# Convolution of the state-space layer: four full products against four half-width products of two taps each

## The chip, the cores and the metric

One core of one Trainium2 chip runs the whole kernel. The metric is the device time of one execution in microseconds (us); lower is better. All data are f32.

## The reference

The input is `x` of 8 sequences, 512 steps, 256 features. Two layers follow each other, each `x = x + s * silu(ffn-like gate)`. The first layer holds the part that changes: a bidirectional state-space block (both directions `d`) beside a mixture of experts.

```
xz = (hidden @ W_in.T).transpose(0, 2, 1)            # per sequence: 1024 channels x 512 steps
x, z = split(xz)                                      # 512 channels each
x = silu(conv(x, conv_w, padding left 3, per channel) + conv_b)     # 4 taps
x_dbl = x @ Wx.T ;  dt = softplus(x_dbl[:64] @ Wdt.T + bdt) ; B, C = rest
h[t] = exp(dt[t] * A) * h[t-1] + dt[t] * B[t] * x[t]  # 512 channels x 16 states
y[t] = C[t] . h[t] + x[t] * D ;  out = y * silu(z)
out_b: the same on the reversed sequence with weights of its own
```

The convolution is per channel: each output is the sum of four shifted inputs, each with one weight. The second layer (linear attention, a three-level MLP, a low-rank gate) is not touched.

## The kernel before

The kernel has three blocks that follow each other: the routing of the experts (first 84 us of the profile), the block with the state-space layer and the experts (84 to about 2,210 us), and the second layer.

In the middle block each sequence `b` has two **units**, `d = 0` (forward) and `d = 1` (backward). A unit has 16 steps `n`, one for each state, and each step has two halves `j`, so 32 **slots** `s = 2n + j`. The order on every engine is written out by hand, slot by slot, and the engines meet at semaphores:

- GpSimd (POOL) makes `dt*B*x` for one state into one of four buffers `hs` (L708), and for two of the 16 states also multiplies by C and adds (L677, L690, L694).
- ScalarE (ACT) makes the decay `exp(dt*A)` into PSUM (`decay`, L797: two instructions per slot, three steps ahead). It may begin only when VectorE has finished the scan that used that half's PSUM buffer.
- VectorE (DVE) runs the scan of a half (L884), two steps ahead, and then adds two turned chunks, weighed by C, to the result (`weigh`, L894).
- TensorE (PE) turns the finished states (`turn`, L1013: transposes into the PSUM banks `hT`), and VectorE's L894 reads them.

Beside this, in chosen slots (`PREP`), TensorE and ScalarE prepare the next unit. While a `d = 1` unit runs, the next sequence's forward unit is prepared: `proj` (L981) in slots 0, 1, 6, 7, each one block `k` of 128 channels, `conv` (L987) in slots 2, 4, 8, 10, then `silu`, `xd`, `dt`. While a `d = 0` unit runs, `conv` for the backward unit of the same sequence is in slots 4, 6, 7, 8 and there is no `proj` (slots 20 to 25 hold `gate`). The one PSUM bank `prep` serves all of these: TensorE waits, before it fills it, until ScalarE has read its last content (`pe.wait_ge(p_used, use)`). In a slot ScalarE's order is: decay, prepare, the expert tile's piece, `skip` (L805), output; TensorE's is: turn, prepare, the tile's piece.

`xpad` is the input of the convolution: 128 channels on the partitions, four blocks, 512 steps with three zeros on each side. ScalarE copies each `proj` result into it (L750). `taps` holds for each direction, block and tap a 128x128 matrix with the tap's weights on its diagonal, built by VectorE at the start of the block (L869). A block of the convolution is four products with the same PSUM target, one for each tap; the shift is the column at which `xpad` is read. The first unit is prepared ahead of all slots, in the same order, with four PSUM banks in turn (`first`).

Of the kernel before, what the change touches and what calls it, by code (L numbers as in the profile page):

```python
# [5 lines left out]
P = 128  # L6
NB, L, DM = 8, 512, 256
DI, NS, R, KC = 512, 16, 64, 4
# [8 lines left out]
DB = DI // P  # L17
HB = HE // P
HF = DB // 2
EPS = 1e-5  # L20
# [11 lines left out]
CW = 0  # L32
CB = CW + 2 * DB * KC
# [35 lines left out]
def bass_mamba_moe_then_linear_attention_mlp(nc, x, w_inT, w_xT, w_dtT, w_outT, cols0, rows0, w_rT, wl1, bl1c, wl2, bl2,  # L69
# [4 lines left out]
    ALU = mybir.AluOpType  # L74
    ACT = mybir.ActivationFunctionType
# [14 lines left out]
    with ctx:  # L90
# [9 lines left out]
        ident = sb("ident", [P, P])  # L100
# [97 lines left out]
        def s0(name, shape, dt=f32):  # L198
            return sb(name, shape, dt, lay0)
# [5 lines left out]
        cols = s0("cols", [P, NCOL0])  # L205
        xa = held[:, :].rearrange("p (c d) -> p c d", d=DM)
# [3 lines left out]
        w_sem = sem("weights_in")  # L210
        N_W = 6
# [5 lines left out]
        with layR:  # L217
# [21 lines left out]
            own = sr("own", [P, NT, NE])  # L239
# [13 lines left out]
            def _(sp):  # L253
# [16 lines left out]
                sp.dma_start(cols[:, :], cols0).then_inc(w_sem, 16)  # L270
                for d in range(2):
                    sp.dma_start(w_x[:, d, :, 0:RX], w_xT[d].rearrange("(k p) m -> p k m", p=P)).then_inc(w_sem, 16)
# [161 lines left out]
        with lay0:  # L434
            one_row = s0("one_row", [1, P])
            xnT = s0("xnT", [P, KD, L])
            xpad = s0("xpad", [P, DB, L + 2 * (KC - 1)])
# [7 lines left out]
            taps = s0("taps", [P, 2 * DB * KC, P])  # L445
# [21 lines left out]
            xnT_in, p_ps, p_used = sem("xnT_in"), sem("prep_ps"), sem("prep_used")  # L467
# [48 lines left out]
            assert N_USE == len(USES[1])  # L516

# [212 lines left out]
            def _(act):  # L730
# [13 lines left out]
                def prepare(what, k, d, unit, b=0, first=False):  # L744
# [4 lines left out]
                    if what == "proj":  # L749
                        nc.scalar.activation(xpad[:, k, KC - 1:KC - 1 + L], src[:, :], ACT.Copy).then_inc(p_used, 1)  # L750
# [110 lines left out]
            def _(dve):  # L861
# [95 lines left out]
            def _(pe):  # L957
# [4 lines left out]
                def prepare(what, k, d, unit, b, first=False):  # L962
# [19 lines left out]
                    elif what == "conv":  # L982
                        if first and k == 0:
                            pe.wait_ge(taps_ready, 2 * DB * KC)
# [630 lines left out]
```

## Time and profile before

| | us |
|---|---|
| median of 3 runs | 3241.3 (3237.01 to 3243.83) |
| the profiled execution, its own time | 3248.7 |
| its span, first to last instruction | 3246.9 |
| busy: PE / DVE / ACT / POOL | 2737.8 / 2252.4 / 1765.3 / 1754.2 |
| mean granted TensorE clock | 0.914 of 2.4 GHz |

Each engine works in its own order, and waits only where its next instruction needs a semaphore. Busy shares are means over three very different blocks, so they say little of one slot. A matmul of f32 appears as two records. In the rows, a bracket gives the idle time before an instruction and what ended it.

### The profile page before, as it was taken

To read this page: it belongs to the slowest core of one execution; us is meant where nothing else is said; L and a number is where in the kernel's file an instruction comes from. 1 tells how busy PE (TensorE), PEld (TensorE's weight loads), DVE (VectorE), ACT (ScalarE), POOL (GpSimd) and SP (SyncE) were. 2 spreads that over 40 slices of the span, in tenths; PEclk is the share of its full clock that TensorE was granted. 3 is DMA by queue.
4 is the path that set the end of the run, shared out by engine and by line. 5 is a ranking of instruction groups with operands and counts; after the bars stand their busy time and mean duration, and the time that the engine had idled before them with its cause. 6 is when DMAs were issued, how large, how long until landed. Compare 5 with 4: busy or idle time off the path is not lost. (4 is left out here: it accounts for less than half of the span.)

```text
span 3246.9 us, 40447 instructions
## 1 busy us (share of the span) xinstructions
PE 2737.8 (84%) x13486; PEld 1826.9 (56%) x13486; DVE 2252.4 (69%) x2812; ACT 1765.3 (54%) x2691; POOL 1754.2 (54%) x554
## 2 busy tenths in 40 slices
PE   5466887887888888878968878777999999999999
PEld 5134665665666565666656656555455555555554
DVE  5287989889889989989988988984442442442430
ACT  1355767758848758758758767641332332322322
POOL 0598868878878878778778887861000000000000
PEclk9777898899999989989989989887999999999999
DMA  6222324333333334333333332323000000000000
GB/s 254 85 69 94 119 101 140 108 109 119 123 106 121 107 104 147 109 105 117 129 115 115 111 134 90 130 89 131 26 33 0 32 32 0 32 18 15 6 7 7
DMA packets 149278, 283.24 MB, mean 87 GB/s; under 512 B 23659, under 2 KB 97878, under 8 KB 149078
## 3 DMA queue, kind: packets, MB, share of 16 engines
q1 hardware_dynamic: 142934, 264.08, 23.8%
q0 software_dynamic: 6144, 16.79, 1.5%
q8 instruction: 91, 1.49, 0.2%
q14 instruction: 109, 0.89, 0.1%
HBM read 239.13 MB, written 41.68 MB: 86 GB/s over the span
## 5 line engine op out<-in xcount | busy, mean ns | idle before, releaser
L708 POOL TENSOR_TENSOR hs<-u,bb 128x2048 f32<-128x2048 f32 x256 | 1159.3, 4534 | 368.5 <-PE hT L1013 323.3
L884 DVE TENSOR_TENSOR_SCAN hs<-dA,hs 128x1024 f32<-128x1024 f32 x512 | 1166.3, 2284 | 122.7 <-POOL hs L708 75.9
L797 ACT ACTIVATE dA<-dt,cols 128x511 f32<-128x511 f32 x1024 | 661.8, 680 | 412.9 <-DVE hs L884 408.6
L1013 PE MATMUL hT<-ident,hs 128*128 128x128 f32 x3584 | 558.4, 297 | 264.2 <-DVE held L894 222.4
L1013 PEld LDWEIGHTS hT<-ident,hs 128*128 128x128 f32 x3584 | 434.9, 151 | 405.6 <-DVE held L894 290.2
L894 DVE SCALAR_TENSOR_TENSOR held<-hT,ct,held 128x512 f32<-128x512 f32 x864 | 603.8, 742 | 54.2 <-PE hT L1013 53.1
L1287 ACT ACTIVATE gl<-bank,cols_sb 128x512 f32<-128x512 f32 x192 | 130.7, 687 | 528.4 <-PE bank L1526 528.1
L1526 PE MATMUL bank<-mT,cms_sb 128*128 128x512 f32 x768 | 363.6, 598 | 10.1 <-ACT mT L1281 8.6
L1032 PE MATMUL moe<-xgT,held 128*128 128x128 f32 x2400 | 334.4, 299 | 30.0 <-ACT xgT L811 28.2
L1032 PEld LDWEIGHTS moe<-xgT,held 128*128 128x128 f32 x2400 | 321.3, 214 | 61.4 <-ACT xgT L811 37.6
L136 POOL COPY cur<-slot 128x8 uint32 (+1 forms) x8 | 1.5, 187 | 640.9 <-DVE held L148 631.3
L1537 PE MATMUL bank<-gl,cms_sb 128*128 128x512 f32 x512 | 242.2, 600 | 7.3 <-issue 3.8
L1526 PEld LDWEIGHTS bank<-mT,cms_sb 128*128 128x128 f32 x768 | 144.4, 191 | 164.7 <-issue 147.5
L987 PE MATMUL prep<-xpad,taps 128*128 128x512 f32 x480 | 219.7, 600 | 2.7 <-ACT xc L758 2.7
L1038 PE MATMUL moe<-held,sa 128*128 128x256 f32 x600 | 178.8, 452 | 8.1 <-DVE sa L904 8.1
L1354 DVE TENSOR_TENSOR sm<-bank,mask 128x512 f32<-128x512 f32 x128 | 82.5, 686 | 137.0 <-PE bank L1421 136.2
L797 ACT ACT_TABLE_LOAD x131 | 168.1, 1283 | 3.7 <-issue 1.4
L1038 PEld LDWEIGHTS moe<-held,sa 128*128 128x128 f32 x600 | 136.6, 236 | 44.8 <-issue 16.2
L981 PE MATMUL prep<-xnT,w_in 128*128 128x512 f32 x248 | 134.8, 672 | 27.7 <-DMA xnT<-xnT_scratch 17.5
L1537 PEld LDWEIGHTS bank<-gl,cms_sb 128*128 128x128 f32 x512 | 92.9, 190 | 114.3 <-issue 101.2
L677 POOL TENSOR_TENSOR hs<-hs,cb 128x2048 f32<-128x2048 f32 x32 | 145.7, 4553 | 0.0
L987 PEld LDWEIGHTS prep<-xpad,taps 128*128 128x128 f32 x480 | 87.5, 192 | 91.8 <-issue 88.6
(219 smaller groups left out, 3332.1 us busy)
## 6 DMA issues: line engine op xcount, KB each, us to landing
held<-wl SPq DMA_DIRECT2D x75, 1024.0 KB
bb<-b_scratch SPq DMA_DIRECT2D x128, 512.0 KB, 5.6
held<-wl SPq DMA_DIRECT2D x75, 512.0 KB
xg_scratch<-zero SPq DMA_DIRECT2D x10, 960.0 KB, 5.4
xg<-xg_scratch SPq DMA_DIRECT2D x75, 128.0 KB
yg_scratch<-yg SPq DMA_DIRECT2D x75, 128.0 KB, 1.7
held<-x SPq DMA_DIRECT2D x16, 512.0 KB, 8.7
cb<-b_scratch SPq DMA_DIRECT2D x32, 256.0 KB, 4.7
```

What stands on the lines that cost most here:

```text
L677: nc.gpsimd.tensor_tensor(hs[m % HS][:, :, :], hs[m % HS][:, :, :], row, ALU.mult).then_inc(p_mul, 1)
L708: nc.gpsimd.tensor_tensor(hs[n % HS][:, :, :], u[d][:, :, :], row, ALU.mult).then_inc(dBu_ready, 1)
L797: last = nc.scalar.activation(dst, src, ACT.Exp, scale=cols[:, at:at + 1])
L884: nc.vector.tensor_tensor_scan(h, decay, h, 0.0, ALU.mult, ALU.add).then_inc(scan_done, 1)
L894: ins = nc.vector.scalar_tensor_tensor(out=yacc[:, c, :], in0=hT[c % 2][:, :], scalar=ct[d][:, c, n:n + 1], in1=yacc[:, c, :], op0=ALU.mul ...
L981: last = mm(dst[:, :], w_in[:, j, at:at + P], xnT[:, j, :], start=(j == 0), stop=(j == KD - 1))
L987: last = mm(dst[:, :], taps[:, (d * DB + k) * KC + t, :], xpad[:, k, at:at + L], start=(t == 0), stop=(t == KC - 1))
L1013: last = nc.tensor.transpose(hT[c % 2][:, k * P:(k + 1) * P], hs[n % HS][:, k, c * P:(c + 1) * P], ident[:, :])
L1032: last = mm(moe[:, m * P:(m + 1) * P], w1[r][:, k, (at + m) * P:(at + m + 1) * P], xgT[:, k, :], start=(k == 0), stop=(k == KD - 1))
L1038: mm(moe[:, 0:DM], sa[:, m, :], w2[r][:, m, :], start=(m == 0), stop=False)
L1526: last = mm(bank[4 + h % 2][:, :], cms1_sb[:, lv, k, h * P:(h + 1) * P], mT[lv][:, k, :], start=(k == 0), stop=(k == KD - 1))
L1537: last = mm(bank[6 + k][:, :], cms2_sb[:, lv, h, k * P:(k + 1) * P], gl[h % 2][:, :], start=(h == 0), stop=(h == HM - 1))
```

## The change

Each product now takes two taps and makes 64 output channels. The input is held twice: `xpad[g]` has on the 64 partitions of half `g` the channels of half `g`, and on the other 64 partitions the same channels, read one step on. A product over all 128 partitions with a 128x64 matrix of two diagonals so gives two taps. ScalarE writes all this from PSUM: four copies of 64 partitions each in place of one of 128. The two halves `g` write the PSUM partitions 0 to 63 and 64 to 127 of the same bank.

```
-            xpad = s0("xpad", [P, DB, L + 2 * (KC - 1)])
+            xpad = [s0(f"xpad{g}", [P, DB, L + 2 * (KC - 1)]) for g in range(2)]
-            taps = s0("taps", [P, 2 * DB * KC, P])
+            taps = s0("taps", [P, 2, DB, 2, KC // 2, HP])

                     if what == "proj":
-                        nc.scalar.activation(xpad[:, k, KC - 1:KC - 1 + L], src[:, :], ACT.Copy).then_inc(p_used, 1)
+                        for g in range(2):
+                            own, other = slice(HP * g, HP * (g + 1)), slice(HP * (1 - g), HP * (2 - g))
+                            nc.scalar.activation(xpad[g][own, k, KC - 1:KC - 1 + L], src[own, :], ACT.Copy)
+                            last = nc.scalar.activation(xpad[g][other, k, KC - 2:KC - 2 + L], src[own, :], ACT.Copy)
+                        last.then_inc(p_used, 1)

-                nc.vector.memset(xpad[:, :, 0:KC - 1], 0.0).then_inc(hT_used, 1)
-                nc.vector.memset(xpad[:, :, KC - 1 + L:], 0.0).then_inc(hT_used, 1)
+                for g in range(2):
+                    nc.vector.memset(xpad[g][:, :, :], 0.0).then_inc(hT_used, 1)
                 dve.wait_ge(w_sem, 16 * N_W)
-                for i in range(2 * DB * KC):
-                    nc.vector.tensor_scalar(taps[:, i, :], ident[:, :], cols[:, CW + i:CW + i + 1], None, ALU.mult).then_inc(taps_ready, 1)
+                for d in range(2):
+                    for k in range(DB):
+                        for g in range(2):
+                            for q in range(KC // 2):
+                                for half in range(2):
+                                    rows_ = slice(HP * half, HP * (half + 1))
+                                    at = (d * DB + k) * KC + tap_of(d, q, int(half != g))
+                                    nc.vector.tensor_scalar(taps[rows_, d, k, g, q, :], ident[rows_, rows_], w_tap[rows_, g, at:at + 1],
+                                                            None, ALU.mult).then_inc(taps_ready, 1)

-                        for t in range(KC):
-                            at = t if d == 0 else 2 * (KC - 1) - t
-                            last = mm(dst[:, :], taps[:, (d * DB + k) * KC + t, :], xpad[:, k, at:at + L], start=(t == 0), stop=(t == KC - 1))
+                        for q in range(KC // 2):
+                            at = pair_at(d, q)
+                            for g in range(2):
+                                last = mm(dst[HP * g:HP * (g + 1), :], taps[:, d, k, g, q, :], xpad[g][:, k, at:at + L],
+                                          start=(q == 0), stop=(q == KC // 2 - 1))
```

`pair_at(d, q)` gives the column at which pair `q` is read, and `tap_of` which tap's weight belongs to which half of the partitions. The weights on both halves come by four small loads into `w_tap` on SP's queue, in the routing block; the count of weight loads that the engines wait for at the start goes from 6 to 10. The number of products of a block stays four.

## Rows read from the trace of the kernel before

**Rows 1.** Page, part 1: busy us of the engines over the span.

```profile
PE 2737.8 (84%) x13486; PEld 1826.9 (56%) x13486; DVE 2252.4 (69%) x2812; ACT 1765.3 (54%) x2691; POOL 1754.2 (54%) x554
```

**Rows 2.** Costliest group by line: busy us, mean ns of one, idle before by releaser.

```profile
L884 DVE TENSOR_TENSOR_SCAN hs<-dA,hs 128x1024 f32<-128x1024 f32 x512 | 1166.3, 2284 | 122.7 <-POOL hs L708 75.9 <-ACT dA L797 33.5 <-issue 12.4
```

**Rows 3.** Waits from 400 to 2150 us: us in total, times, longest.

```profile
ACT xc L758 <- PE prep L987: 50.5, 46, 2.4
...
DVE held L894 <- PE hT L1013: 46.5, 48, 2.6
```

**Rows 4.** Line L750 by itself: ns min/median/max, first and last start.

```profile
L750 ACT ACTIVATE xpad<-prep x30: 574/597/602, 91.5 to 1849.1; 128x512 f32<-128x512 f32 x30
```

**Rows 5.** Timeline of ScalarE, 1316 to 1440 us (a `d = 1` unit), slots 0 to 10.

```profile
1320.77 0.60 ACT L750 ACTIVATE xpad<-prep 128x512 f32<-128x512 f32 x1 [0.61 <-PE prep L981]
1321.27 0.38 ACT L811 ACTIVATE xgT<-moe 128x256 f32<-128x256 f32 x1
...
1322.36 1.30 ACT L797 ACTIVATE dA<-dt,cols 128x511 f32<-128x511 f32 x2
1323.60 0.60 ACT L750 ACTIVATE xpad<-prep 128x512 f32<-128x512 f32 x1
...
1328.58 1.30 ACT L797 ACTIVATE dA<-dt,cols 128x511 f32<-128x511 f32 x2
...
1348.25 1.30 ACT L797 ACTIVATE dA<-dt,cols 128x511 f32<-128x511 f32 x2
...
1356.76 0.69 ACT L758 ACTIVATE xc<-prep,cols 128x512 f32<-128x512 f32 x1 [1.34 <-PE prep L987]
...
1380.84 1.30 ACT L797 ACTIVATE dA<-dt,cols 128x511 f32<-128x511 f32 x2 [0.88 <-DVE hs L884]
```

**Rows 6.** Timeline of VectorE in the same unit.

```profile
1325.83 1.41 DVE L894 SCALAR_TENSOR_TENSOR held<-hT,ct,held 128x512 f32<-128x512 f32 x2
...
1331.46 2.28 DVE L884 TENSOR_TENSOR_SCAN hs<-dA,hs 128x1024 f32<-128x1024 f32 x1
...
1344.80 2.29 DVE L884 TENSOR_TENSOR_SCAN hs<-dA,hs 128x1024 f32<-128x1024 f32 x1 [0.86 <-POOL hs L708]
1347.01 1.38 DVE L894 SCALAR_TENSOR_TENSOR held<-hT,ct,held 128x512 f32<-128x512 f32 x2
...
1351.81 2.28 DVE L884 TENSOR_TENSOR_SCAN hs<-dA,hs 128x1024 f32<-128x1024 f32 x1
```

**Rows 7.** Timeline of TensorE in the same unit.

```profile
1321.68 1.88 PE L981 MATMUL prep<-xnT,w_in 128*128 128x512 f32 x4
...
1325.19 1.04 PE L1013 MATMUL hT<-ident,hs 128*128 128x128 f32 x8
1326.06 3.60 PE L987 MATMUL prep<-xpad,taps 128*128 128x512 f32 x8
1329.50 1.03 PE L1013 MATMUL hT<-ident,hs 128*128 128x128 f32 x8
```

**Rows 8.** Timeline of TensorE in the last block, around a product group of 32 columns.

```profile
2505.04 1.88 PE L1526 MATMUL bank<-mT,cms_sb 128*128 128x512 f32 x4
2506.85 1.08 PE L1434 MATMUL bank<-sm,vp 128*32 128x128 f32 x32
2507.86 1.99 PE L1543 MATMUL bank<-cms_sb,gl 128*128 128x256 f32 x8
```

**Rows 9.** Timeline of 1210 to 1228 us, a `d = 0` unit.

```profile
1214.60 0.69 ACT L758 ACTIVATE xc<-prep,cols 128x512 f32<-128x512 f32 x1 [0.80 <-PE prep L987]
...
1215.80 1.29 ACT L797 ACTIVATE dA<-dt,cols 128x511 f32<-128x511 f32 x2
...
1227.23 2.29 DVE L884 TENSOR_TENSOR_SCAN hs<-dA,hs 128x1024 f32<-128x1024 f32 x1 [3.83 <-POOL hs L708]
```

**Rows 10.** Timeline of 84 to 94 us, the start of the block.

```profile
85.66 0.91 DVE L864 MEMSET dA<- 128x1024 f32 x1 [0.16 <-issue]
...
86.70 6.40 DVE L869 TENSOR_SCALAR taps<-ident,cols 128x128 f32<-128x128 f32 x31
```

More of the change, by code:

```diff
@@ L19 @@
 HF = DB // 2
+HP = P // 2
 EPS = 1e-5
@@ L205, in bass_mamba_moe_then_linear_attention_mlp @@
         cols = s0("cols", [P, NCOL0])
+        w_tap = s0("w_tap", [P, 2, CB])
         xa = held[:, :].rearrange("p (c d) -> p c d", d=DM)
@@ L210, in bass_mamba_moe_then_linear_attention_mlp @@
         w_sem = sem("weights_in")
-        N_W = 6
+        N_W = 10
         placed, zeroed, grouped = sem("placed"), sem("zeroed"), [sem("grouped_early"), sem("grouped_late")]
@@ L270, in _ @@
                 sp.dma_start(cols[:, :], cols0).then_inc(w_sem, 16)
+                for g in range(2):
+                    for half in range(2):
+                        sp.dma_start(w_tap[HP * half:HP * (half + 1), g, :], cols0[HP * g:HP * (g + 1), CW:CB]).then_inc(w_sem, 16)
                 for d in range(2):
@@ L516, in bass_mamba_moe_then_linear_attention_mlp, with pair_at, tap_of @@
             assert N_USE == len(USES[1])
+            def pair_at(d, q):
+                return 2 * q if d == 0 else 2 * (KC - 1) - 1 - 2 * q
+            def tap_of(d, q, early):
+                return pair_at(d, q) + early if d == 0 else 2 * (KC - 1) - pair_at(d, q) - early
             first_banks = [prep, moe, hT[0], hT[1]]
@@ L864, in _ @@
                     nc.vector.memset(dA[j][:, :, :], 0.0).then_inc(scan_done, 1)
-                nc.vector.memset(xpad[:, :, 0:KC - 1], 0.0).then_inc(hT_used, 1)
-                nc.vector.memset(xpad[:, :, KC - 1 + L:], 0.0).then_inc(hT_used, 1)
+                for g in range(2):
+                    nc.vector.memset(xpad[g][:, :, :], 0.0).then_inc(hT_used, 1)
                 dve.wait_ge(w_sem, 16 * N_W)
-                for i in range(2 * DB * KC):
-                    nc.vector.tensor_scalar(taps[:, i, :], ident[:, :], cols[:, CW + i:CW + i + 1], None, ALU.mult).then_inc(taps_ready, 1)
+                for d in range(2):
+                    for k in range(DB):
+                        for g in range(2):
+                            for q in range(KC // 2):
+                                for half in range(2):
+                                    rows_ = slice(HP * half, HP * (half + 1))
+                                    at = (d * DB + k) * KC + tap_of(d, q, int(half != g))
+                                    nc.vector.tensor_scalar(taps[rows_, d, k, g, q, :], ident[rows_, rows_], w_tap[rows_, g, at:at + 1],
+                                                            None, ALU.mult).then_inc(taps_ready, 1)
                 dve.wait_ge(setup_a, 1)
@@ L983, in prepare @@
                         if first and k == 0:
-                            pe.wait_ge(taps_ready, 2 * DB * KC)
-                        for t in range(KC):
-                            at = t if d == 0 else 2 * (KC - 1) - t
-                            last = mm(dst[:, :], taps[:, (d * DB + k) * KC + t, :], xpad[:, k, at:at + L], start=(t == 0), stop=(t == KC - 1))
+                            pe.wait_ge(taps_ready, 4 * DB * KC)
+                        for q in range(KC // 2):
+                            at = pair_at(d, q)
+                            for g in range(2):
+                                last = mm(dst[HP * g:HP * (g + 1), :], taps[:, d, k, g, q, :], xpad[g][:, k, at:at + L],
+                                          start=(q == 0), stop=(q == KC // 2 - 1))
                     elif what == "xd":
```

## The prediction

> **What bounds the kernel now.** I read the page's busy times first [rows 1]. No engine is full over the span, but TensorE at 84% leads, which would make a cheaper convolution look good. That share is a mean over three blocks, so I went to the groups by line. The dearest work of the middle block is VectorE's scan: 1166.3 us busy and only 122.7 us idle before it [rows 2]. The waits from 400 to 2150 us say who makes VectorE idle: TensorE's turned chunks cost it 46.5 us in 48 waits, while ScalarE's 50.5 us of waiting for the convolution [rows 3] is idle time of an engine that is not the bound by itself. So the question is not how much TensorE saves, but whether a slot of VectorE ends earlier or later. For that I read the timelines of one `d = 1` unit [rows 5 to 7] and one `d = 0` unit [rows 9]. A slot of VectorE is a scan and two weighed chunks, 3.5 us (from 1344.80 to 1351.81 are two slots) [rows 6], with almost nothing between. Thus anything that makes a decay or a turned chunk later than its slot stretches the unit, and anything that only makes TensorE earlier does nothing.
>
> **Convolution, cost of a block.** Now it is 8 records; the next turn starts 3.44 us after the first of them (1326.06 to 1329.50) [rows 7], so one record streams in 0.43 us. After the change it is again 8 records of 512 columns. The price hangs on whether the two halves run at once. The trace has no product of 64 columns, but it has one of 32, with four targets in turn: 32 records of 128 columns, and the next group starts 1.01 us after the first [rows 8]. A record of 128 columns one after the other would take 0.43/4 = 0.107 us, so 32 would take 3.4 us; the rows say 3.4 at a time out of four possible. Bounds: 8 x 0.43 = 3.44 us if the halves do not overlap, 4 x 0.43 = 1.72 us if they overlap fully. I take 1.8, since the row of the 32 columns is the same kind of product. Saving: 1.6 us for each of 64 blocks (16 units of four), 105 us of TensorE.
>
> A rule that speaks against this: the Trainium skill (TensorEngine Tiling (Array Packing), Key Properties) says that a change of the tiling mode drains TensorE, and each block now changes it twice. By the trace the change is small: the four records of 512 columns before the narrow group end their streaming at 2505.04 + 1.71 = 2506.75, and the group starts at 2506.85 [rows 8], so 0.1 us. With a drain as large as a record (0.43 us, twice) the saving would fall to 0.8 us a block, and the sum below would hardly move, because the saving is not on the path.
>
> **Copies of the input.** ScalarE writes four copies of 64 partitions where it wrote one of 128. One takes 597 ns [rows 4], and the instruction behind one starts 0.50 us after it (1320.77 to 1321.27) [rows 5]. All still have 512 elements for each partition. No row has a copy of 64 partitions, nor one that lands on other partitions. Bounds: 0.25 us each if the work went by partitions, 0.60 if nothing overlapped; I take 0.50, the row of the same length. So one `proj` costs 3 x 0.50 = 1.5 us more, 32 of them 48 us of ScalarE. Where do these lie? Four per forward unit, in slots 0, 1, 6, 7 of the `d = 1` unit before, seven times in the slots, and once ahead of them.
>
> **Slots 0 to 5 of a `d = 1` unit.** First copies at 1320.77: they end 1.5 us later, and the decay of slot 1 (1322.36) moves by 1.4. Its idle time before was 0.1. The second copies (1323.60) so start 1.4 late and end 2.9 late. Nothing on ScalarE between there and the decay of slot 2 waits for anything, so that decay starts at 1331.5 and ends at 1332.8 instead of 1329.9 [rows 5]. The scan that needs it ran at 1331.46 [rows 6]: it is 1.35 us late. On TensorE, the second `proj` (1321.68) needs the bank that the first copies have to leave: it moves to 1322.9, by 1.2 us, and the turn behind it with it (1325.19) [rows 7]. VectorE's chunk at 1325.83 started at once when its turn was there [rows 6], so it is 1.2 late too. This does not add to the 1.35: it is caught up by the shorter convolution before the next turn (1326.4 + 0.9 + 1.8 = 1329.1, before the old 1329.50). So the change costs 1.35 us here, and the saving on TensorE is what keeps it from being more.
>
> **Slots 6 to 10.** VectorE then waited 0.86 us for GpSimd at 1344.80 [rows 6]. GpSimd's chain to that point does not hang on VectorE's place, so 0.86 of the 1.35 is swallowed: 0.5 left. But the third and fourth copies come in slots 6 and 7. The same count: TensorE's fourth `proj` waits for the third copies, ScalarE's fourth set starts at 1345.8 and ends at 1347.9, the table load, the four Silu, and the table load back follow (3.6 us), and the decay of slot 8 ends at 1352.8, not 1349.5 (1348.25 + 1.25) [rows 5]. Its scan was at 1351.81 [rows 6]: 1.0 late. TensorE's turn of slot 8 comes 2.2 later, behind `proj` and the expert tile, and the chunk that ran at 1347.01 is 1.1 late. So the unit is 1.1 us behind at slot 10.
>
> **The rest of the unit.** With the last convolution ended sooner, ScalarE does not wait 1.34 us for it at 1356.76 and enters the long stretch of `silu`, `xd`, `dt` about 0.3 us earlier. That stretch ends in a wait of 0.88 us for the scan at 1380.84 [rows 5], so the gain becomes more waiting there, and VectorE, without a pause till then, keeps its 1.1. Seven such units: 7 x 1.1 = +7.7 us.
>
> **`d = 0` units.** No copies; the convolution gets shorter in slots 4, 6, 7, 8. ScalarE waited 0.80 us for the first one (1214.60), and behind it stand `skip` and then GpSimd's sum, for which VectorE waited 3.83 us at 1227.23. This looks like a gain of 0.8, but the decay at 1215.80 [rows 9] can't start before its scan ends at about 1215.7. So 0.1 us is left, 0.7 for seven units. I book -0.5.
>
> **Start of the block.** Two memsets of 4 x 518 = 2072 elements each, at 0.91 us for 1024 [rows 10], 1.85 each: 3.7 us. The taps: 31 of 128 elements in 6.40 us, 0.2 each [rows 10]; 64 of 64 elements cost 6.4 us (half the time each) to 13 us (the same each); I take 0.134 each, 8.6 us. TensorE's first convolution starts when they are done, near 99, 6 us late. Its four blocks give back 4 x 1.6 = 6.4, and the third and fourth copies (2 x 1.5, behind each other) stand between; the memsets end before the first copy (91.5). I get +0.5; bounds -3 (if the taps take half) and +7 (if the halves do not overlap). The four small loads lie in the routing block, which ends by VectorE's work; nothing.
>
> **Sum.** 7.7 - 0.5 + 0.5 = +7.7 us on the profiled execution's own 3248.7 us (span 3246.9); that is 0.2% over the median of the runs. On the median: 3241.3 + 7.7 = 3249. A change of 0.2% (6.5 us) is about what this kernel's measurement can tell.
>
> **Rivals.**
> 1. *Swallowed.* The copies pipeline better than 0.50 us, or GpSimd's 0.86 us takes more of the delay. At 0.35 each, the decay of slot 2 ends 2.0 us later, against 1.58 us of room (1331.46 less 1329.88) [rows 5, 6]: 0.4 late, and swallowed at 1344.80. The one of slot 8 ends 2.3 later against 2.3 of room. Some 0.2 is left: 7 x 0.2 = +1.5, so 3243. For it: ScalarE idles before several decays; against it: the row of 0.50. Chance 0.30.
> 2. *Faster.* A TensorE that is 1.6 us sooner in eight slots of 64 takes away VectorE's waits for turned chunks. All of those are 46.5 us [rows 3]; if a fifth lay behind convolutions and went, -9 us: 3232. It decides if more than 1.1 us a sequence goes. Against it: in both units I followed, the waits behind a convolution are 0.7 and 0.3 us and are swallowed later. Chance 0.10.
> 3. *The halves do not overlap.* The convolution stays at 3.44. Then nothing is caught up: 2.4 us in each `d = 1` unit (TensorE hands over the last block 2.4 late, and ScalarE's stretch starts with it), 17 us, and 6.4 at the start: 3265. Rows 8 speak against it. Chance 0.07.
> 4. *TensorE's clock.* The convolution's 0.43 us for a record in slot 2 is that of the higher level, 2.4 GHz, while TensorE worked without a hole [rows 7]. The new holes of 1 to 2 us may bring stretches at 1.2 GHz, in which a turn of 1.04 us takes 2.08. One such turn before a chunk in each of 14 units is about +11 to +14 beside the forecast's: near 3262. Chance 0.08.
>
> The forecast keeps 0.45. Its own range, with the copies at 0.45 to 0.60 us and the start's bounds, is 3244 to 3257. To leave out no more than 2 in 10, I go from 3234, into the faster case, to 3266. Faster by over 0.2%: 0.09. Slower: 0.33 of the forecast's 0.45 lies above 3247.8, with rivals 3 and 4: 0.48. Within 0.2%: 0.43.
>
> **What would show it.** In the changed kernel's trace: L987's successor starts about 1.8 us after the block's first record, not 3.4. Four copies of about 0.6 us each, 0.50 apart, in slots 0, 1, 6, 7. VectorE's wait for ScalarE's decay new in slots 4 and 10 of `d = 1` units, some 1 us; its wait for GpSimd at slot 8 gone. `d = 1` units about 1 us longer, `d = 0` the same. ScalarE's 50.5 us of waiting for the convolution [rows 3] mostly gone and replaced by waiting for scans. I am wrong if copies of 64 partitions pipeline otherwise, or if the start moves by more than 6 us.

## The result

The changed kernel takes 3273.3 us (median; 3273.2 to 3282.2 in 4 runs) against 3240.6 us (3237.0 to 3243.8 in 4 runs) for the kernel before: ratio 1.0107, 95% interval 1.0089 to 1.0124. It is slower by 32.6 us, where the forecast said 7.7. The direction was right; the time lies above the range.

In the profiled executions (spans 3246.9 and 3280.4 us; both are some 8 to 9 us over the median of their kernel) the loss is in two places:

| stretch, by VectorE's scans | before | after | |
|---|---|---|---|
| start to the first scan | 157.4 | 176.8 | +19.4 |
| fifth scan (slot 0 of the first unit) to the last | 2007.2 | 2022.1 | +14.9 |
| behind the last scan | 1068.4 | 1067.5 | -0.9 |

(Between the first and the fifth scan both need 14.0 us.) A `d = 1` unit, from the scan of slot 0 to that of slot 31, mean of six units (the first is left out), takes 119.9 us in place of 117.5; with the first, 119.8 in place of 117.6. A `d = 0` unit, from the scan of slot 1 to the first scan of the next unit, takes 124.1 in both. So 7 x 2.2 = 15.1 us is the whole of the middle, and the start is somewhat larger. Within the unit the loss lies between the scans of slots 0 and 12: 45.9 us in place of 43.4, mean of all seven. Slots 12 to 19 take 24.4 us in both kernels, slots 19 to 31 take 49.6 in the changed one and 49.8 before.

### The profile page after: what moved, and what is told of

The parts are those of the page before. It is cut to its first block and busy times, and to the rows that moved or that the text cites. A ratio compares the mean times of both kernels' runs of the same rounds, so it can differ in the third digit from the quotient of the medians.

```text
span 3280.4 us, 40579 instructions
## 1 busy us (share of the span) xinstructions
PE 2667.5 (81%) x13486; PEld 1768.3 (54%) x13486; DVE 2267.5 (69%) x2844; ACT 1822.2 (56%) x2787; POOL 1754.7 (53%) x554
## 5 line engine op out<-in xcount | busy, mean ns | idle before, releaser
L1042 PE MATMUL hT<-ident,hs 128*128 128x128 f32 x3584 | 567.9, 299 | 310.3 <-DVE held L921 267.8
L1015 PE MATMUL prep<-xpad,taps 128*64 128x512 f32 x480 | 118.6, 615 | 13.5 <-ACT xc L778 13.5
L1356 DVE TENSOR_TENSOR vp<-bank,vmask 128x256 f32<-128x256 f32 x64 | 24.2, 420 | 142.0 <-PE bank L1502 141.6
```

The source lines that it names most:

```text
L1042: last = nc.tensor.transpose(hT[c % 2][:, k * P:(k + 1) * P], hs[n % HS][:, k, c * P:(c + 1) * P], ident[:, :])
```

## The profile after

Page of the changed kernel, parts 1 and 5, against [rows 1, 2]:

```profile
PE 2667.5 (81%) x13486; PEld 1768.3 (54%) x13486; DVE 2267.5 (69%) x2844; ACT 1822.2 (56%) x2787; POOL 1754.7 (53%) x554
...
L911 DVE TENSOR_TENSOR_SCAN hs<-dA,hs 128x1024 f32<-128x1024 f32 x512 | 1166.3, 2284 | 125.0 <-POOL hs L724 68.5
```

TensorE has 70 us less to do and the kernel is 33 us slower; ScalarE has 57 us more. Waits of the changed kernel, 400 to 2150 us, against [rows 3]:

```profile
DVE held L921 <- PE hT L1042: 55.2, 45, 2.7
...
DVE hs L911 <- ACT dA L817: 42.4, 26, 3.8
DVE hs L911 <- POOL hs L724: 31.2, 14, 4.3
```

ScalarE's 50.5 us of waiting for the convolution is not in the list any more, as forecast; VectorE's wait for turned chunks went from 46.5 to 55.2. Where these lie is seen in a `d = 1` unit. TensorE, against [rows 7]:

```profile
1350.31 1.98 PE L1008 MATMUL prep<-xnT,w_in 128*128 128x512 f32 x4 [1.17 <-ACT xpad L769]
...
1353.91 1.04 PE L1042 MATMUL hT<-ident,hs 128*128 128x128 f32 x8
1354.88 1.94 PE L1015 MATMUL prep<-xpad,taps 128*64 128x512 f32 x8
1356.74 1.09 PE L1042 MATMUL hT<-ident,hs 128*128 128x128 f32 x8
```

The block of the convolution, from its first record to the next turn, is 1.86 us (1354.88 to 1356.74), where it was 3.44. The turn in front of it now takes 0.97 us to the block's start (1353.91 to 1354.88), where it took 0.87 (1325.19 to 1326.06) [rows 7]. But the second `proj` stands 1.17 us waiting for the bank. ScalarE in slots 1 and 2 of the same unit, against [rows 5]:

```profile
1352.39 0.58 ACT L768 ACTIVATE xpad<-prep 64x512 f32<-64x512 f32 x1
1352.99 0.59 ACT L769 ACTIVATE xpad<-prep 64x512 f32<-64x512 f32 x1
1353.59 0.60 ACT L768 ACTIVATE xpad<-prep 64x512 f32<-64x512 f32 x1
1354.20 0.60 ACT L769 ACTIVATE xpad<-prep 64x512 f32<-64x512 f32 x1
1354.81 1.28 ACT L836 ACT_TABLE_LOAD   x1
```

The copies start 0.60 us apart, not 0.50: a set of four takes 2.42 us (1352.39 to 1354.81). VectorE in slots 2, 4, 8 and 10, against [rows 6]:

```profile
1354.55 1.41 DVE L921 SCALAR_TENSOR_TENSOR held<-hT,ct,held 128x512 f32<-128x512 f32 x2 [1.43 <-PE hT L1042]
...
1360.60 2.29 DVE L911 TENSOR_TENSOR_SCAN hs<-dA,hs 128x1024 f32<-128x1024 f32 x1 [1.14 <-ACT dA L817]
...
1376.25 1.41 DVE L921 SCALAR_TENSOR_TENSOR held<-hT,ct,held 128x512 f32<-128x512 f32 x2 [0.97 <-PE hT L1042]
...
1381.63 2.29 DVE L911 TENSOR_TENSOR_SCAN hs<-dA,hs 128x1024 f32<-128x1024 f32 x1 [0.47 <-ACT dA L817]
```

Two pairs of waits, each a late turned chunk and then a late decay; GpSimd's wait of [rows 6] between them is gone. VectorE at the start, against [rows 10]:

```profile
86.96 1.78 DVE L886 MEMSET xpad<- 128x2072 f32 x1 [0.42 <-issue]
89.12 1.78 DVE L886 MEMSET xpad<- 128x2072 f32 x1 [0.38 <-issue]
90.82 20.36 DVE L895 TENSOR_SCALAR taps<-ident,w_tap 64x64 f32<-64x64 f32 x64
```

The taps take 20.4 us, though they write half of what they wrote in 6.4: 0.32 us each. TensorE's first convolution runs at 111.33, 18 us later than before.

## The experiments

The kernel before gave 3226.7, 3226.6, 3249.6, 3248.7 and 3239.0 us beside the five sets of runs below (four chips; the third and the fifth set ran on the same one), so each ratio is to the kernel before of the same set. "Backward unit" is the 117.5 us above, the mean of six.

That mean is unsteady, and its scatter goes with TensorE's clock. In the changed kernel slots 19 to 31 take 48.8 to 49.4 us in four units with a granted clock of 0.83 to 0.86 over them, and 50.1 to 50.3 in three units with 0.76; in the kernel before one at 0.86 takes 49.4 and one at 0.76 takes 50.0. So the same code gave backward units of 119.9, 119.8 and 120.6 us in three profiles (the change twice, and the change with its taps in another order), and a difference of less than about 1 us between two such means shows nothing. Steadier is the stretch from the scan of slot 0 to that of slot 12, the mean of all seven units: 43.4 us before, and 45.9, 45.8 and 46.1 in those three. It is given below as "slots 0 to 12".

### First set: the four suspects

**Taps by full height.** The weights of a pair come in one table over 128 partitions, and 32 instructions of 128x64 make all taps.

```
-  for half in range(2):
-      nc.vector.tensor_scalar(taps[rows_, d, k, g, q, :], ident[rows_, rows_], w_tap[rows_, g, at:at + 1], ...)
+  nc.vector.tensor_scalar(taps[:, d, k, g, q, :], id2[:, :], w_tap[:, i:i + 1], ...)
```

> The changed kernel, but VectorE builds the weights of the paired products with 32 instructions of 128 partitions x 64 elements (a doubled 64-wide identity times a column that already holds the weight of either half) in place of 64 of 64 partitions x 64 elements; one load in place of four brings those columns. My theory, that instructions of half height do not overlap with the next one (0.32 us apart against 0.20 for full height): the 32 take 4.3 to 6.4 us, the first scan comes 14 to 16 us earlier than in the changed kernel, and the time is 3257 us, some 16 above the kernel before. Rival, that the start is late by TensorE's late signals to ScalarE and not by the weights: only 5 us or less come back, 3268.

Measured: 3243.2 us, ratio 1.0051 (1.0037 to 1.0065), +16.4. Backward unit 119.8, as in the change; slots 0 to 12 take 46.0. This is the base for most kernels below.

**The kernel before, with its taps by halves.**

```
-  nc.vector.tensor_scalar(taps[:, i, :], ident[:, :], cols[:, CW + i:CW + i + 1], ...)
+  for half in (slice(0, 64), slice(64, P)):
+      nc.vector.tensor_scalar(taps[half, i, :], ident[half, :], cols[half, CW + i:CW + i + 1], ...)
```

> The kernel before, with each of the 32 instructions that build the weights split into its lower and upper 64 partitions (64 instructions of 64 partitions x 128 elements). Theory of no overlap at half height: some 0.38 us apart, 24 us in place of 6.4, and +18 us: 3258. Rival, the price is by elements alone: 0.20 apart, 12.8 us, +6: 3247. Rival, the start hides it: no change.

Measured: 3239.8 us, ratio 1.0041 (1.0026 to 1.0057), +13.1; backward unit 117.4, slots 0 to 12 43.4. The taps, VectorE's timeline at the start (the change with full height, then the kernel before with halves):

```profile
90.97 5.29 DVE L891 TENSOR_SCALAR taps<-id,w_tap 128x64 f32<-128x64 f32 x32
```

```profile
86.63 19.99 DVE L870 TENSOR_SCALAR taps<-ident,cols 64x128 f32<-64x128 f32 x63
```

0.16 us each at full height and 0.32 by halves (the kernel before, at full height, needs 0.20 for its 128 columns). So the halves alone, without any of the rest, make a loss of this size at the start.

**No overlap of the halves.** Both products of a pair go to partitions 0 to 63, so one must follow the other.

```
-  mm(dst[HP * g:HP * (g + 1), :], ...)
+  mm(dst[0:HP, :], ...)            # in all units but the first
```

> As e1_full_height_taps, but in all units except the first both halves of a block are written to PSUM partitions 0 to 63, so that they cannot run at once (the output of the upper 64 channels is left out). Theory, that the halved convolution is what keeps the copies' delay small in the backward units: a block takes 3.44 us again, and each of the seven backward units gets about 1 to 1.5 us longer, the forward ones stay: +7 to +10 us on e1. Rival, that TensorE's saving is worth nothing at all: the same as e1 within 2 us.

Measured: 3259.4 us, ratio 1.0103 (1.0087 to 1.0118), 16.3 over the full-height kernel; backward unit 121.0, slots 0 to 12 47.1, `d = 0` unit 125.6. TensorE's timeline:

```profile
1329.55 3.65 PE L1011 MATMUL prep<-xpad,taps 128*64 128x512 f32 x8
1333.13 1.09 PE L1038 MATMUL hT<-ident,hs 128*128 128x128 f32 x8
```

A block is 3.58 us without overlap and 1.86 with it. The time was lost in both directions, 1.2 us in a backward unit and 1.5 in a `d = 0` unit, about twice what was expected. But this doesn't say what the shorter block gains over the kernel before, whose `d = 0` unit takes 124.1 us with a block of 3.44, as long as with 1.86. What the kernel without overlap has beside it are the longer turn in front of the block (0.97 us to its start, not 0.87 or 0.88) and the 0.14 behind it: some 0.24 us a block. In `d = 0` units they add up: VectorE's wait for the turn in slot 7 is 0.91 us (0.28 in the kernel before), and 0.34 and 0.20 are new in slots 9 and 12. In the change the shorter block covers them.

**Products alone.** One copy as before; the products read it, half of their input not filled.

```
-  (four copies of 64 partitions)
+  nc.scalar.activation(xpad[0][:, k, KC - 1:KC - 1 + L], src[:, :], ACT.Copy).then_inc(p_used, 1)
```

> As e1_full_height_taps, but ScalarE makes only one copy of 128 partitions, into the first of the two inputs, as the kernel before does; the second input stays zero and no shifted copy is made (their part of the output is left out). Theory, that the four copies make all of the loss in the units: backward and forward units as long as before, time 3240 +-5 us, so 13 to 18 under e1. Rival, that the two changes of the tiling per block or a lower clock of TensorE cost: units longer than before by 0.5 us or more, time 3250 or above. Rival, that a cheaper convolution speeds the units up once the copies are gone: under 3232.

Measured: 3224.9 us, ratio 0.9995 (0.9986 to 1.0004), backward unit 117.4, slots 0 to 12 43.6. With everything but the copies, the kernel is where it was: all of the middle's loss is the copies', 18.2 us between this kernel and the full-height one. And the 1.6 us taken out of each of 64 convolutions bring nothing that can be measured: VectorE gains 0.8 us in slot 3 and waits it off for GpSimd by slot 8.

### Second set: why taps and copies cost what they cost

Theory: a VectorE or ScalarE instruction that starts on other partitions than the one before can't begin before that one is finished. Rival: an instruction of 64 partitions is slow by itself.

**Taps by half, in order.** The loop over `half` is put outside, so that it changes once and not 64 times. The changed kernel ran beside it once more.

> The changed kernel with its 64 instructions that build the weights in another order: all 32 of the lower partitions first, then all 32 of the upper, in place of lower and upper in turn. Theory, that an instruction is held until the one before it has finished when it reads or writes from another start partition: the held ones are gone but for one, 0.17 us apart in place of 0.32, 11 us in place of 20.4, and the time 9 to 10 us under the changed kernel. Rival, that half height itself costs the overlap: still 0.32 apart, the same time as the changed kernel.

> The changed kernel as it is, timed on the chip of these runs, so that the others can be set against it. If the weights cost 15 us and the copies 2.4 us in each of seven backward units (16.8), with 4 us given back at the start by the shorter convolution: 15 + 17 - 0 to 2, so 30 to 32 us over the kernel before, as the first measurement had.

Measured: 3248.6 us, ratio 1.0068 (1.0051 to 1.0085), and 3260.6 us, ratio 1.0109 (1.0092 to 1.0126), for the changed kernel, +34.0. The order alone is worth 12.0 us:

```profile
90.86 10.78 DVE L895 TENSOR_SCALAR taps<-ident,w_tap 64x64 f32<-64x64 f32 x64
```

0.16 us each, as the 128 partitions took. The rival falls. In the changed kernel the single instructions show the same: they last 0.25 and 0.40 us, start 0.28 and 0.43 apart, so each starts 0.03 us after the end of the one before. The backward unit of the reordered kernel is 120.6: slots 0 to 12 take 46.1, as in the change, and slots 19 to 31 had the lower clock in all of the last six units.

**Two copies of 128 partitions**, none shifted, and **four copies in an order with one change of partitions** (0 to 63 twice, then 64 to 127 twice, none shifted), both on the full-height kernel.

```
+  for g in range(2):                                           # two full copies
+      nc.scalar.activation(xpad[g][:, k, KC - 1:KC - 1 + L], src[:, :], ACT.Copy)
...
+  for rows_ in (slice(0, HP), slice(HP, P)):                   # same start, twice each
+      for g in range(2):
+          nc.scalar.activation(xpad[g][rows_, k, KC - 1:KC - 1 + L], src[rows_, :], ACT.Copy)
```

> As e1_full_height_taps, but with two copies of 128 partitions, one into each input, in place of four of 64 (the shifted halves of the output are left out). Copies 0.50 us apart by both theories of the hold. Theory of slots: a set ends 0.5 us later than with one copy, the decay of slot 2 about 1.0 us later against 1.58 us of room, the rest is swallowed: backward units as long as before (117.5 us over slots 0 to 30), time within 2 us of e4_products_alone, so about that of the kernel before. Rival, that the loss grows evenly with the copies' time (1.9 us more for a set gives 2.4 us a unit): 0.6 us a unit, +4 us.

> As e1_full_height_taps, four copies of 64 partitions, but each stays on its partitions and the order is lower, lower, upper, upper (no shifted or crossing copy; that part of the output is left out). Theory of the start partition: the second behind the first and the fourth behind the third are 0.50 us apart, the third 0.60; a set takes about 2.2 us. Rival, half height: all 0.60 apart, 2.4 us. By slots the backward units then lose 2.0 to 2.2 us by the first theory, 2.4 by the second; time 12 to 15 us over the kernel before.

Measured: 3226.5 us, ratio 1.0000 (0.9990 to 1.0009), backward unit 117.4, slots 0 to 12 43.4; and 3235.3 us, ratio 1.0027 (1.0017 to 1.0038), 118.6 and 44.9. For the second too much was expected, 12 to 15 us and 2.0 to 2.2 in a unit: it is 8.6, and 1.2. Copies start 0.49 us apart on the same partitions and 0.59 apart where the start changes, so a set is 0.3 us shorter than in the change, and that is worth 1.2 us of a unit. The time isn't made by having two input tiles: half a microsecond more per set costs nothing, 1.6 us cost 1.2 in a unit (1.5 in slots 0 to 12), 1.9 cost 2.4.

### Third set: an attempt to spread the copies

Theory: the loss needs two sets in neighbouring slots. `proj` goes from slots 0, 1, 6, 7 to 0, 3, 6, 9: in the full-height kernel, in the kernel before, and in the first of these with memsets of the edges only.

```
-  plan(0, "proj", (0, 1, 6, 7))
+  plan(0, "proj", (0, 3, 6, 9))
```

> As e1_full_height_taps (four copies, full result), with the four input projections in slots 0, 3, 6, 9 in place of 0, 1, 6, 7, so that no two sets of copies follow each other. Theory, that the loss comes from two sets in a row in front of the decays of slots 2 and 8: ScalarE then has at most 5.5 us of work in a slot and catches up in the next, backward units lose 0.5 us or less in place of 2.4, and the time is within 4 us of the kernel before. Rival, that each set costs its 1.9 us wherever it is: no change from e1_full_height_taps, +16.

> The kernel before with the projections in slots 0, 3, 6, 9. It tells what the move does by itself. I expect within 2 us of the kernel before: nothing waited for the old places. Rival: the move gives a gain or loss of its own, 5 us or more.

> As e8_spread_proj, and VectorE clears only the edge columns of the two inputs (four memsets of a few columns) in place of both inputs in full, ahead of the weights at the start. The two full memsets took 3.7 us: the first scan comes about 3.5 us earlier than in e8_spread_proj, and the time is 3 to 4 us lower. With the start then some 7 us earlier than in the kernel before, and units as long, it is 3 to 7 us under the kernel before. Rival, the start is bound by the projection's result (its copy began at 91.4 us) and not by the weights: nothing, or under 1 us.

Measured: 3285.6 us, ratio 1.0111 (1.0096 to 1.0125); 3265.1 us, ratio 1.0052 (1.0040 to 1.0064); 3282.5 us, ratio 1.0099 (1.0084 to 1.0113). None of the three expectations held (within 4 us of the kernel before, within 2, and 3 to 7 under it). VectorE in slot 4, first in the full-height kernel with the spread, then in the kernel before with it:

```profile
1359.57 1.13 DVE L926 SCALAR_TENSOR_TENSOR sa<-moe,b,sa 128x128 f32<-128x128 f32 x4 [2.12 <-PE moe L1056]
```

```profile
1342.56 1.13 DVE L904 SCALAR_TENSOR_TENSOR sa<-moe,b,sa 128x128 f32<-128x128 f32 x4 [1.05 <-PE moe L1032]
```

In slots 3 and 9 TensorE has a piece of the expert tile behind its preparation, and `proj` ahead of it made that late. The spread costs the kernel before 15.6 us by itself. Counted from the scan of slot 0 to that of slot 19, it takes the kernel before from 67.8 to 69.8 us, and the copies on top make it 70.8; without the spread they make it 70.3. So copies in slots that aren't neighbours cost 0.9 us a unit on top and not 2.5, but the spread itself costs 2.0, more than the 1.6 that it saves.

The edges' memsets didn't do what was expected. TensorE's first convolution starts 2.7 us earlier with them (93.7 for 96.4), but the fifth scan is at 184.2 and 184.0, so nothing is won at the start. The 3.2 us between the medians are as much as the last unit differs in the two profiles (its 32 scans take 116.9 and 120.1); without the memsets it is 116.9 with two full copies and 120.2 in the change, so no run shows that the memsets shorten it.

### Fourth and fifth set: which queue

Two queues stretch behind a set of copies: TensorE's, since the bank is handed back late, and ScalarE's own, in which the decay stands behind the copies. **Bank early** frees the first alone: the two copies that stay on their partitions come first, the bank goes back, then the shifted ones are made from SBUF (these start 0.64 us apart, so a set is 0.1 us longer). **Late shifts** frees mostly the second: the shifted copies of blocks 1 and 3 move to slots 3 and 9. It has memsets of the edges only. The full-height kernel ran beside them.

```
   for g in range(2):
       last = nc.scalar.activation(xpad[g][own, ...], src[own, :], ACT.Copy)
   last.then_inc(p_used, 1)                                     # bank early
+  act.wait_ge(p_used, use + 1)
+  for g in range(2):
+      last = nc.scalar.activation(xpad[g][other, ...], xpad[g][own, ...], ACT.Copy)
+  last.then_inc(shifted, 1)
...
+  PREP[0][3].append(("late", 1));  PREP[0][9].append(("late", 3))   # late shifts
```

> The changed kernel with full-height taps once more (32 products of 128x64, as in the first run of this kind), so that the next two can be read against it on one chip. Expected by its first run: about 0.5% over the kernel before, +16 us; VectorE's slots 0 to 30 of a backward unit 119.8 us against 117.4.

> The changed kernel with full-height taps, but ScalarE makes the two copies that stay on their partitions first, hands the bank back to TensorE after those two (1.2 us instead of 2.4), and then makes the two shifted copies from the input tiles in SBUF. ScalarE's own work is as long as before. Theory A (ScalarE is what binds: its decays of slots 2 and 8 come 1.8 us late because two sets of copies stand ahead of them): the turned chunks are no longer late in slots 2 and 8 (VectorE's 1.5 us wait for TensorE goes), the wait for the decay grows by about as much, and slots 0 to 30 of a backward unit stay at 119.8 within 0.3 us; the time stays within 3 us of the run with full-height taps. Theory B (the bank binds: the turn behind the held-up projection is what is late): a backward unit loses 1 us or more of its 2.4, slots 0 to 30 at or under 118.8, the time 7 us or more lower.

> The changed kernel with full-height taps, with memsets of the edges only, and with the two shifted copies of blocks 1 and 3 taken out of slots 1 and 7 and made from SBUF in slots 3 and 9, behind the decays of slots 2 and 8, where ScalarE has room; blocks 0 and 2 as in the change. The same number of copies, only later. Theory A (ScalarE's queue in slots 0 to 2 and 6 to 8 binds): 1.2 us less stand ahead of the decays of slots 2 and 8, so a backward unit loses 0.2 to 0.8 us instead of 2.4 and slots 0 to 30 come to 117.6 to 118.3; with some 4 us less of memsets at the start the time is 12 to 18 us under the run with full-height taps, near the kernel before (-4 to +4 us). Theory B (the number of copies or TensorE's mode changes cost the time wherever they lie): slots 0 to 30 stay above 119, and only the memsets' 4 us come back.

Measured, in this order: 3266.5 us, ratio 1.0059 (1.0046 to 1.0073); 3268.2 us, 1.0066 (1.0052 to 1.0079); 3271.0 us, 1.0072 (1.0058 to 1.0085). Backward units 119.8, 119.9 and 119.7; slots 0 to 12 take 45.9, 46.0 and 46.4. Three kernels with one loss, made by different waits. VectorE with the early bank, then with the late shifts:

```profile
1346.69 2.29 DVE L911 TENSOR_TENSOR_SCAN hs<-dA,hs 128x1024 f32<-128x1024 f32 x1 [2.67 <-ACT dA L821]
```

```profile
1349.26 1.41 DVE L927 SCALAR_TENSOR_TENSOR held<-hT,ct,held 128x512 f32<-128x512 f32 x2 [1.23 <-PE hT L1050]
...
1363.86 1.41 DVE L927 SCALAR_TENSOR_TENSOR held<-hT,ct,held 128x512 f32<-128x512 f32 x2 [2.09 <-PE hT L1050]
```

The early bank leaves 0 to 0.9 us of the wait for the turn in slot 2 (1.2 to 1.7 us in the full-height kernel, from the second unit on), and the wait for the decay grows from 1.14 to 2.67: the 1.5 us that VectorE first waited for TensorE it now waits for ScalarE. With the late shifts no wait for a decay is left in these slots, but the bank still is late in slot 2, and a new one stands in slot 6: the second block's convolution waits for its late copies,

```profile
1357.10 2.48 PE L1023 MATMUL prep<-xpad,taps 128*64 128x512 f32 x8 [2.77 <-ACT xpad L778]
```

and the turn behind it is late. In slot 8 VectorE's wait for the turn is 1.75 us, where it was 0.97. My expectation of the late shifts (117.6 to 118.3) failed: the decays were cured and nothing was won. For the bank alone the proof is less clean than for ScalarE's queue, because of the new wait in slot 6; in the three units in which it is only 0.45 us, slots 0 to 12 still take 45.4 to 45.6.

**Both together**, and the same with the edges' memsets: own copies first, then the shifted ones of block 0 in slot 1, of block 1 in slot 2, of block 2 in slot 7, of block 3 in slot 9.

```
+  PREP[0][1].append(("late", 0));  PREP[0][2].insert(0, ("late", 1))
+  PREP[0][7].append(("late", 2));  PREP[0][9].append(("late", 3))
```

> Both cures at once on the changed kernel with full-height taps: the bank goes back to TensorE after the two unshifted copies, and the shifted copies are made from SBUF, those of block 0 behind the unshifted of block 1 (slot 1), of block 1 in slot 2 behind the decay, of block 2 in slot 7, of block 3 in slot 9. Memsets as in the change. Theory A (either queue alone is enough to make the 2.4 us; so the cures must come together): the second projection comes 0.6 us late instead of 1.8, the decays of slots 2 and 8 2.4 us instead of 3.6, against 1.6 and 2.3 us of room, so slots 0 to 30 of a backward unit come to 117.5 to 118.6, and the stretch of all units to 2008 to 2016 us, against 2024 with full-height taps. Theory B (the number of copies costs the time wherever they lie): slots 0 to 30 at 119.5 or more.

> The same with memsets of the edges of the input only, which ends the taps some 4 us sooner. Expected: the units as in the run beside it; the time up to 4 us under it, less where TensorE waits for the input at the start anyway. Against the kernel before, by theory A: 0 to 8 us over it down to 4 under.

Measured: 3253.8 us, ratio 1.0045 (1.0030 to 1.0059); 3269.7 us, ratio 1.0094 (1.0079 to 1.0109). In the first the backward unit is 118.6, slots 0 to 12 take 45.1, and the stretch of all units is 2015.7 us against 2023.8 of the full-height kernel: half of the loss is gone, as expected where both queues carry it. VectorE in one of its longest units, slots 2, 4 and 6:

```profile
1333.47 1.41 DVE L926 SCALAR_TENSOR_TENSOR held<-hT,ct,held 128x512 f32<-128x512 f32 x2 [0.47 <-PE hT L1049]
...
1339.46 2.29 DVE L916 TENSOR_TENSOR_SCAN hs<-dA,hs 128x1024 f32<-128x1024 f32 x1 [1.08 <-ACT dA L826]
...
1348.25 1.41 DVE L926 SCALAR_TENSOR_TENSOR held<-hT,ct,held 128x512 f32<-128x512 f32 x2 [1.11 <-PE hT L1049]
```

The wait for the turn in slot 2 is smaller, the one for the decay in slot 4 nearly what it was, and the one in slot 6 is that of the late shifts. But the mean hides two kinds of unit. In two of the seven, slots 0 to 12 take 43.5 us, as in the kernel before: there nothing of the copies' loss is left, and the granted clock over the stretch is 0.97. In the other five they take 45.2 to 46.5, with a granted clock of 0.89 to 0.92. The convolution in slot 4, in a unit of the first kind and in one of the second:

```profile
833.95 1.94 PE L1022 MATMUL prep<-xpad,taps 128*64 128x512 f32 x8 [2.92 <-ACT xc L787]
```

```profile
1086.28 3.68 PE L1022 MATMUL prep<-xpad,taps 128*64 128x512 f32 x8 [2.93 <-ACT xc L787]
```

The same 2.9 us of idle TensorE stand before both, but the granted clock is 1.00 (2.4 GHz) from 833.9 to 836 and 0.50 (1.2 GHz) from 1086 to 1090. Behind the slow block VectorE waits 2.35 us for the turn in slot 6, behind the fast one it doesn't wait. In this profile and in that of the second kernel of this set, the block takes 1.94 us in all four short units and 3.1 to 3.7 in all ten long ones. In the change, where the hole in front of it is 1.5 us, it takes 1.94 in all seven. So what is left goes with the lower clock behind the longer hole, and not with the two queues. Why the clock fell in one unit and not in the other was not tested.

The second missed: 15.9 us over the first instead of up to 4 under. Its units are the same: slots 0 to 12 take 45.0, in two units 43.4 at a clock of 0.97, in the other five 45.2 to 46.4 at 0.89 to 0.92. The fifth scan comes at 179.0 against 172.9, though its taps were done 4.2 us earlier (92.1 against 96.3): ScalarE's two long waits for TensorE at the start are 7.45 and 16.92 us, and 5.40 and 11.49 in the first. What makes these is open. The two profiles differ by 8.5 us, and that of the second is its fastest execution. No version with the four copies beats the kernel before.

## Why the forecast missed

Two terms of the sum failed, both too small. The start of the block was booked at +0.5 us, with the taps at 0.134 us each; they took 0.32, and the start lost some 17.5. The copies were taken at 0.50 us apart and 7.7 us in all; they were 0.60 apart and cost 15.1. The path that was forecast, copies ahead of the decays of slots 2 and 8, was the right one.

**Convolution, cost of a block.** Forecast 1.8 us, measured 1.86. The 32-column row carried over to 64 columns. Four records of 0.43 are 1.72, so 0.14 us are left behind the block, and the turn in front of it takes 0.10 us longer to the block's start. That is an estimate of 0.24 us for the two changes of the tiling mode: the forecast's 0.1 for one, read from [rows 8], was right, and the 1.8 has room for one of them only. Rival 3 (no overlap) is out.

**Copies of the input: the first term that was mis-sized.** 0.50 us apart were taken from a row in which the next instruction started on the same partition; 0.60, the upper bound, is what came. The mechanism behind it held, as the forecast's own working shows at 0.60. A set takes 2.42 us, 1.9 more than a copy's 0.50, and two sets 3.8. The decay of slot 2 had 1.58 of room: 2.2 late; measured 1.9 (slots 2 and 3 took 9.84 us for 7.93). GpSimd's wait swallowed 1.0 (0.86 forecast), 0.9 left. The second pair: 3.8 less 2.3 of room, plus the 0.9: 2.4 late. Measured 2.4 a unit in slots 0 to 12, where 1.1 was said, and 15.1 us in all seven units, where 7.7 was said; the 1.7 between 7 x 2.4 and 15.1 lies in slots 19 to 31, where the changed kernel's profile by luck has more units at the higher clock. A tenth of a microsecond in each of 16 copies of a unit cost 1.3 us of the unit, since the room was used up by the first 0.50. The order with one change of partitions (118.6) shows the same slope from the other side.

**"TensorE's bank wait does not add".** Right in the sum, but it isn't second in rank: ScalarE's queue alone makes the whole loss, which the early bank shows, and the bank nearly alone, which the late shifts show. And the faster convolution did keep the loss from being more: 1.2 us in a backward unit by the kernel without overlap, where the forecast had 1.3 (2.4 less 1.1). The 1.5 us of a `d = 0` unit, for which it had nothing, are not a gain over the kernel before but the price of the narrow products without overlap.

**`d = 0` units.** Booked -0.5 us, measured no change (124.1 us in both).

**Start of the block: the second, larger term.** Memsets 3.7 us forecast, 2 x 1.78 measured. The taps were taken at 0.134 us each with 0.2 as the upper bound; they took 0.32, outside the bounds. The bound assumed that half an instruction costs no more than a whole one. It left out that an instruction which changes its start partition waits for the one before. In the profiles this is the better part of the +19.4 of the start; by the medians it is 12.0 us for the order alone and some 17.5 for by-halves against full height (34.0 less 16.4, of two sets whose kernels before agree within 0.1 us). Were only the start right, the forecast would have missed by some 7 us; were only the copies right, by 17. The working has a slip too: 6 us late, less 6.4, plus 3.0 are +2.6 and not the +0.5 booked.

**Rivals.** Swallowed (3243): what it needed, 0.35 us between copies, is far off; but the mechanism was real: with two full copies all was swallowed. Faster (3232): the products alone gave 0.9995, so no fifth of VectorE's waits lay behind convolutions. TensorE's clock (3262): the granted clock from 400 to 2210 us is 0.90 in both kernels, and over slots 0 to 12 of the unit followed here, where the loss is, it is 0.96 in both, so no. But such stretches at the lower clock do cost time here: the scatter of slots 19 to 31 goes with them, and so does what is left when both queues are cured.

**The range** ended at 3266, with the start's worst case at +7. The two sure losses are alike in kind, both from the row of a neighbour on the same partitions, and the range took them as independent. The forecast's "own range" to 3257 was too short even for its own bounds: copies at 0.60 give 2.4 us a unit by its working, 17 in seven, and with +7 at the start that is near 3265.

## What to carry to other kernels

Halving the height of an instruction halved nothing here on VectorE or ScalarE (a copy takes 0.594 us for 64 partitions and 0.597 for 128), and alternating between start partitions takes the overlap of neighbours away: order such a series by start partition, or lay the data out so that it runs over all 128. Before a cheaper product is bought with more copies, read how much room the decays and banks behind those copies have; past it, each tenth of a microsecond counts once per copy. If two queues run out of room in the same place, curing either alone shows nothing, so an experiment on one of them that moves no time does not acquit it. And look at units one by one before a mean is explained: the same kernel had units of 116.7 and 120.7 us.

## What the runs showed of the hardware that was not expected

- VectorE: `tensor_scalar` on 64 columns starts every 0.163 us while the start partition stays, on 128 or on 64 partitions, and 0.28 to 0.43 us apart where it alternates between 0 and 64, 0.03 us after the end of the one before. The Trainium skill (VectorE: DVE Perf Modes, Two Vector instructions with no wait between them) says that an instruction whose input or output starts in another quadrant than that of the last one on the same memory starts only when all earlier ones are done. The runs agree, the reordered taps most plainly.
- ScalarE: copies of 512 elements start 0.493 us apart on the same partitions, and 0.59 to 0.60 where the start changes, which is the copy's own duration. Line L769 of the changed kernel:

```profile
L769 ACT ACTIVATE xpad<-prep x60: 589/594/597, 92.0 to 1884.8; 64x512 f32<-64x512 f32 x60
```

  The Trainium skill (ScalarE: Activation LUTs, What ACT_TABLE_LOAD costs) gives an overlap of about 93 ns for neighbours. The trace is near it for the same partitions (0.597 less 0.493, 0.104 us); it is gone where they change.
- TensorE's granted clock was 0.50 of 2.4 GHz behind some holes of 2.9 us and 1.00 behind others of the same length, in one kernel with both cures; the block behind them took 3.68 and 1.94 us. Units of that kernel took 116.7 to 120.7 us.
- The start differs between chips. ScalarE in the changed kernel's profile waits there, by the program for TensorE's products, and TensorE has nothing in its row meanwhile (the profile names no instruction, only `remote`):

```profile
128.80 0.69 ACT L778 ACTIVATE xc<-hT,cols 128x512 f32<-128x512 f32 x1 [13.06 <-remote]
135.10 0.59 ACT L768 ACTIVATE xpad<-prep 64x512 f32<-64x512 f32 x1 [5.61 <-remote]
```

  The kernel before has 8.49 and 12.95 us of the same. In the eight profiles of the first two sets, beside which it took 3226.7 and 3226.6 us, there are none; each of the eight profiles of the other sets has 17 to 26 us of such waits. What TensorE does in these stretches was not found. Since their length differs from profile to profile, the +19.4 us of the start are only a rough measure; the medians within a set are the better one.
